# Zero matmuls in the counting loops of a graph network kernel: kept in the loop by eight chunks, taken out of the loop by four

## The reference

```python
edge_index = jnp.stack([src, dst])
x = _layernorm(x + _L0_gnn_ref(x, ..., src, dst))
x = _layernorm(x + _L1_gnn_ref(x, edge_index, ...))
x = _layernorm(x + _L2_gnn_ref(x, edge_index, ...))
x = _layernorm(x + _L3_gnn_ref(x, ..., src, dst))
```

## Time and profile before

| | |
|---|---|
| three runs | 1942.35 us median (1939.85 to 1944.84) |
| the profiled execution | 1943.61 us, of which the span of the instructions is 1941.8 |
| TensorE busy | 1751.3 us, 90% of the span |
| mean granted clock | 0.962 |
| counting stage | about 34 to 352 us |

### The profile page before, as it was taken

The page is one execution under the profiler, slowest core; times in us unless marked ns, Lnnn a source line. Parts: engine busy times, 40 slices in busy tenths (PEclk is TensorE's granted clock), DMA queues, the critical chain, the costliest instruction groups (busy, mean ns, idle before and its releaser), DMA issues.

```text
span 1941.8 us, 35011 instructions
## 1 busy us (share of the span) xinstructions
PE 1751.3 (90%) x9445; PEld 1414.8 (73%) x9479; DVE 952.7 (49%) x2851; ACT 482.4 (25%) x1262; POOL 495.3 (26%) x899
## 2 busy tenths in 40 slices
PE   3888888599988999999999999999999699999971
PEld 2355555488878888888888887887777489898951
DVE  7876665344445521112221117776767544444466
ACT  0134445322223311122221111112122132223223
POOL 1122222311113300000000001225888843232314
PEclk7999999699999999999999999999999899999986
DMA  5188999899969989866667988887877399999981
GB/s 134 34 273 297 321 323 329 308 325 327 321 214 369 360 283 292 287 214 214 209 203 276 293 288 278 288 291 235 265 253 260 133 300 372 371 371 372 371 313 66
DMA packets 269052, 535.59 MB, mean 276 GB/s; under 512 B 17871, under 2 KB 195322, under 8 KB 265242
## 3 DMA queue, kind: packets, MB, share of 16 engines
q1 hardware_dynamic: 259114, 516.24, 79.1%
q0 software_dynamic: 7888, 17.23, 2.4%
q10 hardware_dynamic: 1952, 0.95, 0.3%
HBM read 405.95 MB, written 128.41 MB: 275 GB/s over the span
## 4 chain that ended last, share of the span: by engine, by line
PE 68%; POOL 10%; DMA 7%; issue 5%; DVE 5%; SPq 3%; DVEq 2%; ACT 1%; ACTq 0%; POOLq 0%
PE psum L1109 39%; PE psum L592 7%; PE psum L604 6%; DMA blk<-counts_src_on_rows 4%; PE psum L1001 4%; PE psum L1206 3%; PE psum L998 3%; POOL expert_rows_in L1979 3%; POOL pick_and_gate_of_row L1996 2%; PE psum L1020 2%; SPq L827 1%; PE psum L1217 1%; PE psum L1188 1%; DMA expert_weights<-expert_rows_out 1%; DMA counts_src_on_rows<-blk 1%
## 5 line engine op out<-in xcount | busy, mean ns | idle before, releaser
L1109 PE MATMUL psum<-xsa,blk 128*128 128x512 f32 x2500 | 637.2, 403 | 11.7 <-DVE xsa L1675 9.7
L1109 PEld LDWEIGHTS psum<-xsa,blk 128*128 128x128 f32 x2500 | 456.7, 189 | 98.4 <-issue 12.6
L1109 PE MATMUL psum<-xsb,blk 128*128 128x512 f32 (+1 forms) x1875 | 406.1, 366 | 12.2 <-DMA blk<-counts_src_on_rows 9.2
L1109 PEld LDWEIGHTS psum<-xsb,blk 128*128 128x128 f32 x1875 | 315.8, 190 | 64.7 <-issue 10.6
L1957 POOL TENSOR_SCALAR ve<-mv 128x1 f32<-128x1 f32 x75 | 16.8, 225 | 763.1 <-DVE mv L1651 763.1
L1536 DVE TENSOR_SCALAR onehots<-counts_scratch 128x348 bf16<-128x348 f16 x464 | 162.1, 375 | 87.8 <-issue 47.0
L998 PE MATMUL psum<-onehots 128*128 128x349 bf16 x464 | 149.3, 322 | 40.3 <-DVE onehots L1541 38.1
L592 PE MATMUL psum<-route,expert_weights 128*128 128x128 f32 x1296 | 165.2, 281 | 2.2 <-DVE route L704 1.9
L1001 PE MATMUL psum<-zrow 128*128 128x512 bf16 x431 | 164.8, 391 | 0.0
L592 PEld LDWEIGHTS psum<-route,expert_weights 128*128 128x128 f32 x1296 | 152.6, 193 | 12.9 <-DVE route L704 2.6
L604 PE MATMUL psum<-expert_weights,route 128*128 128x256 f32 x648 | 153.2, 380 | 0.4 <-ACT route L658 0.4
(11 more groups left out here) (317 smaller groups left out, 2112.2 us busy)
## 6 DMA issues: line engine op xcount, KB each, us to landing
blk<-counts_src_on_rows SPq DMA_DIRECT2D x125, 832.0 KB
blk<-counts_src_on_rows SPq DMA_DIRECT2D x125, 768.0 KB
expert_weights<-in_L_gnn_w SPq DMA_DIRECT2D x162, 512.0 KB
blk<-counts_dst_on_rows SPq DMA_DIRECT2D x50, 832.0 KB
counts_dst_on_rows<-band_rows SPq DMA_DIRECT2D x25, 1600.0 KB, 8.2
blk<-counts_dst_on_rows SPq DMA_DIRECT2D x50, 768.0 KB
counts_src_on_rows<-blk SPq DMA_DIRECT2D x13, 1600.0 KB, 8.7
counts_src_on_rows<-rblk SPq DMA_DIRECT2D x12, 1600.0 KB, 9.8
```

The costliest lines, as they stand in the source:

```text
L1109: mm = e.matmul(o, blk[n][:, k * P:(k + 1) * P], XS[:, k, :, 0:Fw], start=(k == 0), stop=(k == T - 1 and not own), skip_group_check=True)
```

## The change

The zero matmul behind each chunk is now issued only in the loop by eight. In the loop by four a chunk's matmul stands alone, with the same waits and the same signal. The zero matmuls that open and close a band's sum (L989, L1006) stay, and no other engine's program changes.

```diff
                             e.matmul(o, one_d[:, u, :], one_s[:, u, 0:FW + 1], start=False, stop=True,
                                      skip_group_check=True).then_inc(S("onehots_used"), 1)
 
-                            e.matmul(psum[:, par, 0:BANK], zrow[:, 0:P], zrow[:, 0:BANK], start=False, stop=True,
-                                     skip_group_check=True)
+                            if by > UNROLL:
+                                e.matmul(psum[:, par, 0:BANK], zrow[:, 0:P], zrow[:, 0:BANK], start=False, stop=True,
+                                         skip_group_check=True)
                 groups(before, middle, 2 * UNROLL)
                 side()
                 groups(middle, upto, UNROLL)
```

## The result

| | median us | lowest to highest | runs |
|---|---|---|---|
| before | 1941.46 | 1939.85 to 1944.84 | 4 |
| changed | 1974.74 | 1971.97 to 1980.53 | 4 |

The changed kernel is slower: ratio 1.0174, 95% interval 1.0154 to 1.0193, 33.3 us. Forecast were +22.5 us and a time of 1964.9, in a range of 1943 to 1979: the direction and the mechanism came out, the size was too small by a third.

The account below looks back on a forecast made before the run. The counting stage was taken as bound by a ring TensorE, VectorE, TensorE, once a band. 12 clock falls x 2.95 = 35.4, less 3.9 for three existing falls and 9.0 for 30 turns, made +22.5 us: 1964.9, range 1943 to 1979.

Parts of the forecast that it names:

- The ring: Counting stage: the chain of waits goes TensorE, VectorE, TensorE once a band, so the loop by four is on the path.
- what a turn gains: Loop by four at full clock: each turn without zero matmuls gains 0.30 us; 30 turns, 9.0 us.
- What the removal leaves behind: Around the loop by four: holes of 2.0 us on TensorE, so the clock falls in 12 bands instead of 3.
- case B: Counting stage: the clock falls in nearly every band, 24 falls, +58 us, 2000 us; chance 0.07.
- The price of a fall: Transposes and loop by eight at half clock: each fall costs 2.95 us, between 1.3 and 4.6.
- The sum: Whole kernel: 35.4 for 12 falls, less 3.9 for three already there, less 9.0 for turns: +22.5 us.
- The end of the stage: Two stores behind the last band: they move as one piece with it and hide a loss by 2 us at most.
- D: Counting stage: the clock holds as before and only the gain is left, -3 to -8 us, 1936 us; chance 0.12.
- E: Counting stage: the clock holds and the stores already set the pace, so nothing comes out; chance 0.05.
- C: Counting stage: 3 to 7 clock falls, dearer than before, -4 to +7.8 us; chance 0.10.

Follow-up runs that it names:

- e1_ahead: The changed kernel with six zero matmuls a band put just ahead of the loop by four, in TensorE's idle time: 1937.67 us, 0.9981 of the kernel before.
- e5_three_ahead: The changed kernel with three zero matmuls a band put just ahead of the loop by four: 1939.15 us, 0.9989 of the kernel before.
- e4_narrow: The kernel before with the zero matmuls of the loop by four narrowed from 512 to 256 columns: 1955.04 us, 1.0066 of the kernel before.
- e6_behind: The changed kernel with four zero matmuls a band in a row behind the loop by four: 1970.91 us, 1.0141 of the kernel before.
- e3_no_zeros: The kernel before without zero matmuls in either the loop by four or the loop by eight: 1973.37 us, 1.0169 of the kernel before.

## Why the prediction was right, and where it was off

**The ring, and what a turn gains.** Right for a turn. At full clock a band of 12 chunks went from 9.00 to 8.75 in the changed kernel and to 8.70 in e1_ahead, up to the 0.30 us worked out from VectorE's rows. But the gain is one for each band, not for each turn: in bands 18 and 20, with two turns, e1_ahead gained 0.27 and 0.31. So the term is 25 x 0.30 = 7.5, not 9.0.

**What the removal leaves behind.** The mechanism was right and is shown: e1_ahead has the changed loop by four and no falls, and is 37 us faster. What was mis-sized is the count: 21 falls against the 12 forecast. I had taken a half for holes of 2.0 us because three of six bands with 1.7 or more had held. (One of the 19 others, band 24, had an idle time of 1.12 and not 1.36 or more, which changes nothing here.) With the holes of an ordinary band worked out as in the prediction, the experiments give the scale: no fall with half a microsecond of idle left and holes inside mostly closed up (e1_ahead), 2 with 1.35 us (e5_three_ahead), 3 with 1.4 and up to 2.4 in single bands (before), 10 with 1.6 (e4_narrow), 21 with 2.0 (changed). Each count is of one execution. The hope that 2.0 was still near the middle of this was the error; case B was nearer in count. The sum of the holes is not all of it, since e6_behind has 2.0 and 11 falls.

**The price of a fall.** Too high: 2.95 against 2.1. At the last band the changed kernel is 362.3 - 318.8 = 43.5 us behind e1_ahead, its twin at full clock: over 21 falls 2.07 each. It lies between my bounds of 1.3 and 4.6, and on the low side of the middle. The transposes cost nearly what was said: 1.7 more for sixteen (3.66 against 1.98 in the same view), where the half clock covers all of them. My 1.8 had set a time from one view against one from the chain. In the shorter falls it covers only three to eight of them. The loop by eight cost less than its 2.8, since the clock was back by the fifth of its chunks at the latest. Twelve of the 21 falls lasted only 3.4 us; one of these cost 1.5 (band 10: 13.60 against the 12.10 of e1_ahead's band 12, which has as many chunks), one of the nine that lasted 6.8 cost 3.1 (band 12: 15.25 against 12.10). Twelve and nine at these prices are 46 us, close to the 43.5.

**The sum.** Forecast: 12 x 2.95 - 3.9 - 9.0 = +22.5. With the measured terms: 21 x 2.07 = 43.5, less the 10.4 that e1_ahead ends earlier than before (7.5 for the turns and 3 for the three falls), +33.1 at the last band. This only splits the measured time, since 2.07 comes from it. A count too small and a price too high partly cancelled, and that is luck: with the measured price and my count the sum would have been 12 x 2.07 - 12.9 = +11.9, with the measured count and my price 21 x 2.95 - 12.9 = +49.

**The end of the stage.** Right: it hid none of the loss, 33.1 at the last band and 33.4 at the next stage.

**The rivals.** D, the clock holds, is refuted for the changed kernel, and e1_ahead shows about what D would have been: its median is 5.3 us below that of the kernel before (1 to 6 by the interval), and 3.7 us of its gain at the last band went to the stores, as D said (I had 6 us left). E said that the stores would take all of the gain; e1_ahead speaks against it. C is out by the count of falls. A table of the Trainium skill spoke for D ("TensorE: Matmul & The Clock Gate", Why this matters for your kernels): it warns only of idle gaps longer than any in band 11. As a bound this does not hold here, since no idle was longer than 1.41 us in the turn of band 11, and there the clock fell at 210.4. The other rule of that page (A second HAM failure mode: psum-queue depth-cycling), that frequent small idles between groups of matmuls are enough, agrees with these runs.

**What stays open.** Why the falls come so regularly: from 247 to 344 us each band of the changed kernel has one, and they are alternately 6.8 and 3.4 us long. In e4_narrow, too, the clock fell just behind bands 7, 9 and 11 (158.4, 182.3 and 206.2) and not behind bands 8, 10, 12 or 13, whose turns look alike. So the length of the holes alone does not say which band loses the clock; when the band starts may matter, and no run shifts only that. How holes and the work around them weigh against each other is known only from the points above.

## What to carry to other kernels

A matmul that computes nothing may be holding the clock: before it is taken out, look for the idle time next to it, and price what stands behind it at half clock too. If it must be there, put it where the engine waits anyway; six zero matmuls in the idle time did what four on the path did, for 0.30 us a band less. If the loop next to it is bound by another engine, fillers that keep the clock only part of the time may gain nothing: with the zeros left only in the loop by eight (1974.74 us) or only in the loop by four (1971.94) the kernel was as slow as with none (1973.37).

## What the runs showed of the hardware that was not expected

A stage that was at half clock for most of its time was no slower than one that went up and down: 1973.37 us with a clock of 0.60 from 70 to 318 us, against 1974.74 with 0.83. The first has no zero matmuls that could cost time at half clock.

```profile
70.00:318.00 248.00, 210.24 (x825) 136.13 (x833) 149.61 (x552) 93.02 (x189) 49.07 (x60) 0.60 0.73 245
```

```profile
70.00:318.00 248.00, 210.51 (x1068) 132.53 (x1067) 153.93 (x552) 92.59 (x189) 49.19 (x60) 0.83 0.73 244
```

Each is one window, with columns as above; the first row is of e3_no_zeros, the second of the changed kernel: VectorE ran the same number of instructions, 552, in both.
